# Turned x loaded for seven of eight tile pairs, and tile stores issued by ScalarE, in the front of a fused mixture kernel

## Chip, cores and metric

One Trainium2 chip, one core, one launch. The metric is the device time of the program in microseconds, as the median of several runs. Everything is float32 in memory. TensorE multiplies, VectorE (DVE), ScalarE (ACT) and GpSimd (POOL) do the rest; SyncE (SP) only issues transfers and waits.

## What is computed

```python
def reference(x, cond_128, ...):          # x: [32, 64, 1024], cond_128: [32, 128]
    x = x + L0_ffn(L0_cond(x, cond_128))
    x = x + L1_ffn(L1_cond(x, cond_128))
    return x

def L0_cond(x, emb):                      # mixes the 64 channels of a sample
    h = gelu(emb @ W0 + b0); h = gelu(h @ W1 + b1)
    att = softmax(h @ W2 + b2)            # [32, 8]
    agg_w = einsum('bk,koi->boi', att, weight); agg_b = att @ bias_k
    return einsum('boi,bih->boh', agg_w, x) + agg_b[:, :, None]

def L0_ffn(x):                            # 2048 rows of 1024, 8 experts, 2 of them per row
    topv, topi = top_k(x @ gate_w, 2); w = softmax(topv)
    return sum over the two experts e of w_e * (x @ expert_w[e])

def L1_cond(x, c):                        # grouped convolution, 9 taps, and c @ c_weight.T + bias
def L1_ffn(x):                            # x @ weight.T, and LoRA of 2 of 8 experts chosen by a gate
```

## The kernel before

The 2048 rows (32 samples of 64 channels) are 16 tiles of 128 rows, each with 1024 columns. The program has three parts: the **front** (0 to about 84 us of the profiled execution) mixes the channels, computes the gate, sorts every row into the lists of its two experts and stores the mixed rows in a scratch in DRAM (`c0_d`); the **expert slots** (92 to about 505 us) gather 128 rows of one expert at a time and multiply them with its weights, as three products of rounded parts (a low part of the rows with the high part of the weights, high with high, high with low; line 1498); the **second layer** takes the rest. The change touches the front and the first slot.

The front goes over pairs of tiles, `it` = 0 to 7; pair `it` has tiles `2*it` and `2*it + 1`. Nothing is scheduled by the compiler: each engine runs its own list of instructions in the order written, and they meet at semaphores.

- **x** comes twice. SyncE loads all 16 tiles as they are (`load_x`, line 453, 512 KB each, into `res`, read by the mixing). The gate needs x with columns on the partitions. For the pairs in `LOADED` (2 to 7) a copy turned on the host, `x_t`, is loaded (line 476, 1 MB a pair, into one of two buffers `xt_pair`, pair `it` in buffer `it % 2`). Pairs 0 and 1 are turned on chip: TensorE transposes a quarter of the pair into bank 4 (`turn_x`, line 1356), ScalarE copies it out (`take_turned`, line 755), and only then the next quarter may go in.
- **Prologue.** Three small matmuls with gelu and softmax make the attention (to line 931); TensorE spreads it over the partitions (line 1425), VectorE puts it in place (`att_own`, line 937), and 16 matmuls with `kern_sb` make the 32 mixing matrices in banks 0 to 3 (line 1442). VectorE (line 952) and ScalarE (lines 775, 778) copy them to `bd`, 4 copies each. Besides, lines 1428 to 1431 multiply the column sum of the gate, the context of the second layer and the bias. The column sum comes through `gsum`, the bias through a chain of four VectorE operations to `aggb` (line 948), which ScalarE needs for its first eviction of a mixed tile.
- **Gate.** `gate_products(it)` (line 1370) multiplies the turned pair with the gate's weights into bank 6; VectorE copies it (`take_rows`, line 961); `turn_gate` (line 1382) brings it back to rows, VectorE copies that (line 966), and `logits` (line 1401) mixes it.
- **Mixing.** `mix(it, j, h)` (line 1393) multiplies half `h` of tile `j` of the pair with its mixing matrix; ScalarE adds the bias while copying to `c0_sb[j]` (`take_c0`, line 764), and SyncE stores the tile (line 480).
- **Routing.** VectorE picks the two best logits (`route`), TensorE counts ranks (lines 1408, 1409), VectorE makes one-hot matrices (lines 990, 991), and `lists` (line 1417) adds up the row numbers of each expert's list.
- **Expert 0's weights** come beside this, one eighth in each pair (`load_raw0`, line 457), rounded by ScalarE (line 769), with the remainder taken by VectorE (`rest0`, line 1026).

TensorE's order in a pair is: the gate turn, mixing of tile 0 in two halves, logits, mixing of tile 1 in two halves, lists of the pair before, gate products of the pair after, ranks. In pair 0 the four quarters of pair 1's transposes stand between these.

SyncE's order sets when transfers start: all 16 tiles of x first, with two eighths of expert 0's weights between them; then, in each pair, the turned pair `it + 2` once the gate products of pair `it` have freed its buffer, the two stores once ScalarE has evicted, and an eighth of the weights.

Behind the last lists, GpSimd gathers the first 128 rows (`xg`, line 648), TensorE transposes them into banks 2 and 3 (line 1489), ScalarE rounds each half to `l_hi` (lines 797, 802), VectorE takes the remainder `l_lo` (lines 1086, 1091), and slot 0 begins.

## Time and profile before

| | us |
|---|---|
| median of the runs (807.08 to 810.27) | 807.54 |
| the profiled execution | 806.61 |
| its span in the profile | 804.9 |
| front, up to the first gather | 0 to 84.4 |
| first product of expert slot 0 | 92.0 |
| TensorE busy | 780.9 (97%) |
| VectorE busy | 393.6 (49%) |
| ScalarE busy | 206.3 (26%) |

The profile is one execution. Its page gives busy times of each engine and, in 40 slices, how busy they and the DMA engines were. The chain of waits goes back from the last instruction: at each step to what released it, or to the instruction before it on its engine. The timeline lists instructions in order of time, neighbours of one kind merged; in brackets stands how long the engine was idle before and what ended that. A matmul of float32 appears as two instructions. The granted clock is a separate column, in which 1.00 is full.

### The profile page before, as it was taken

The page shows a single profiled execution, that of the slowest core. Times are in us where ns is not written, and L with a number is a line of the kernel's source. Part 1 is how long each engine was busy: PE and PEld are TensorE (multiplying, and loading weights), DVE is VectorE, ACT ScalarE, POOL GpSimd, SP SyncE. Part 2 cuts the span into 40 slices and gives each one's busy share as a digit, 9 for nine tenths or more (in the row PEclk, how much of TensorE's full clock was granted, in tenths as well). Part 3 has the DMA queues.
Part 4 walks back from the last instruction along what each step waited for, and adds up shares of the span by engine and source line. Part 5 has one row for each costly group of instructions (what it writes and reads, how often), then busy time and mean ns, then how long its engine had stood idle before and what let it go on. Part 6 is the DMA issues. An engine that isn't in the chain of part 4 may idle for free.

```text
span 804.9 us, 13018 instructions
## 1 busy us (share of the span) xinstructions
PE 780.9 (97%) x4426; PEld 635.9 (79%) x4426; DVE 393.6 (49%) x920; ACT 206.3 (26%) x324; POOL 84.7 (11%) x127
## 2 busy tenths in 40 slices
PE   6999899899999999999999999999999999999997
PEld 4555587678787787877878888878988889889886
DVE  2688642330422413214133153475777667778883
ACT  3444152341523314224133251300000010001200
POOL 1000202001110110001011112211111111200000
PEclk9999999999999999999999999999999999999999
DMA  9997397376482765726455355774445654442066
GB/s 349 388 372 264 126 375 259 113 252 244 177 308 95 243 268 196 277 97 224 148 174 199 104 196 175 240 190 115 104 108 143 144 126 104 113 98 52 1 221 197
DMA packets 62880, 152.51 MB, mean 189 GB/s; under 512 B 7148, under 2 KB 24700, under 8 KB 61948
## 3 DMA queue, kind: packets, MB, share of 16 engines
q1 hardware_dynamic: 43152, 99.84, 38.0%
q0 software_dynamic: 9504, 34.48, 14.0%
q10 hardware_dynamic: 10188, 17.71, 5.9%
q8 instruction: 22, 0.36, 0.2%
q14 instruction: 14, 0.11, 0.1%
HBM read 99.04 MB, written 44.57 MB: 178 GB/s over the span
## 4 chain that ended last, share of the span: by engine, by line
PE 90%; DMA 5%; issue 2%; ACT 1%; DVE 1%; SPq 1%; POOLq 0%; POOL 0%; ACTq 0%; DVEq 0%
PE bank L1498 61%; PE bank L1586 6%; PE bank L1595 4%; PE bank L1393 3%; PE bank L1489 3%; PE bank L1541 3%; PE bank L1602 3%; DMA work<-c_scratch,idx 3%; PE bank L1370 1%; PE bank L1417 1%; PE bank L1552 1%; DMA work<-y_scratch,pos_c 1%; DMA x1p<-res 1%; PE bank L1356 1%; PE bank L1382 1%
## 5 line engine op out<-in xcount | busy, mean ns | idle before, releaser
L1498 PE MATMUL bank<-weights,l_hi 128*128 128x512 f32 x1536 | 473.5, 389 | 0.0
L1498 PEld LDWEIGHTS bank<-weights,l_hi 128*128 128x128 f32 x1536 | 288.4, 188 | 58.3
L1498 PE MATMUL bank<-weights,l_lo 128*128 128x512 f32 x768 | 304.7, 397 | 1.1 <-DVE l_lo L1086 1.1
L1498 PEld LDWEIGHTS bank<-weights,l_lo 128*128 128x128 f32 x768 | 144.2, 188 | 34.0 <-issue 6.2
L1086 DVE TENSOR_TENSOR l_lo<-bank,l_hi 128x512 fp32r<-128x512 f32 x32 | 22.2, 693 | 174.7 <-ACT l_hi L797 174.7
L1118 DVE TENSOR_TENSOR weights<-work,weights 128x1024 fp32r<-128x1024 f32 x48 | 55.9, 1221 | 33.9 <-ACT weights L809 33.9
L1586 PE MATMUL bank<-conv_sb,x1p 128*128 128x128 f32 x512 | 59.8, 275 | 2.7 <-DMA x1p<-res 1.6
L1586 PEld LDWEIGHTS bank<-conv_sb,x1p 128*128 128x128 f32 x512 | 58.7, 192 | 3.2 <-DMA x1p<-res 1.8
L1240 DVE TENSOR_TENSOR res<-bank,res 128x512 f32 (+1 forms) x30 | 31.9, 1064 | 54.8 <-PE bank L1498 43.8
L648 POOL DMA_INDIRECT work<-c_scratch,idx x32 | 33.4, 1045 | 227.1 <-PE bank L1489 138.8
L888 ACT ACTIVATE l_hi<-work 128x512 fp32r<-128x512 f32 x32 | 18.4, 623 | 135.4 <-PE bank L1498 129.2
L1091 DVE TENSOR_TENSOR l_lo<-bank,l_hi 128x512 fp32r<-128x512 f32 x32 | 22.1, 692 | 63.1 <-ACT l_hi L802 63.1
L809 ACT ACTIVATE weights<-work 128x1024 fp32r<-128x1024 f32 x48 | 47.2, 1046 | 18.7 <-issue 18.3
L797 ACT ACTIVATE l_hi<-bank 128x512 fp32r<-128x512 f32 x33 | 19.8, 599 | 98.0 <-PE bank L1498 88.5
L841 ACT ACTIVATE work<-bank 128x512 f32<-128x512 f32 x32 | 19.1, 596 | 87.4 <-PE bank L1498 69.0
L1595 PE MATMUL bank<-down_sb,work 128*128 128x160 f32 x256 | 37.4, 299 | 0.6 <-DVE hb L1206 0.6
L1192 DVE TENSOR_TENSOR work<-bank,ctxb 128x512 f32<-128x512 f32 x32 | 33.6, 1131 | 8.5 <-PE bank L1586 7.8
L1595 PEld LDWEIGHTS bank<-down_sb,work 128*128 128x128 f32 x256 | 36.2, 190 | 1.8 <-issue 0.8
L802 ACT ACTIVATE l_hi<-bank 128x512 fp32r<-128x512 f32 x33 | 19.7, 598 | 68.3 <-PE bank L1498 68.3
L1489 PEld LDWEIGHTS bank<-ca,work 128*128 128x128 f32 x264 | 30.8, 140 | 7.7 <-issue 2.2
L1489 PE MATMUL bank<-ca,work 128*128 128x128 f32 x264 | 34.4, 272 | 2.4 <-DMA work<-c_scratch,idx 2.4
L698 POOL DMA_INDIRECT work<-y_scratch,pos_c x32 | 32.8, 1026 | 26.2 <-POOL pos_c L693 9.7
(204 smaller groups left out, 603.6 us busy)
## 6 DMA issues: line engine op xcount, KB each, us to landing
work<-in_expert_w SPq DMA_DIRECT2D x52, 512.0 KB, 5.4
y_scratch<-work ACTq DMA_DIRECT2D x64, 256.0 KB, 3.4
x1p<-in_expert_w SPq DMA_DIRECT2D x20, 512.0 KB, 8.3
y_scratch<-ca SPq DMA_DIRECT2D x19, 512.0 KB, 10.1
res<-in_x SPq DMA_DIRECT2D x16, 512.0 KB, 11.2
c_scratch<-work SPq DMA_DIRECT2D x16, 512.0 KB, 5.0
res<-in_x_ph SPq DMA_DIRECT2D x14, 512.0 KB, 5.8
x1p<-res SPq DMA_DIRECT2D x112, 64.0 KB, 4.7
```

Of the source, the lines that this page charges most:

```text
L648: pool.indirect_dma_start(xg, None, c0_d, bass.IndirectOffsetOnAxis(ap=idx[:, 0:1], axis=0)).then_inc(s_xg, 16)
L698: pool.indirect_dma_start(yg[j][:, k, :], None, y_d, bass.IndirectOffsetOnAxis(ap=pos_c[j][:, k:k + 1], axis=0)).then_inc(s_yg[j][k], 16)
L809: act.activation(w_hi[1 - odd][:, at, :], raw[buffer(at)], ACT.Copy).then_inc(s_hi, 1)
L1118: dve.tensor_tensor(w_lo[1 - odd][:, at, :], raw[buffer(at)], w_hi[1 - odd][:, at, :].bitcast(F32), ALU.subtract).then_inc(s_lo, 1)
L1192: dve.tensor_tensor(out4[:, b], ps, add.unsqueeze(2).to_broadcast([P, CQ, HC, CP]), ALU.add).then_inc(s_c1, 1)
L1240: dve.tensor_tensor(to[:, w, :], bank[h][:, :].rearrange("p (w q) -> p w q", q=PH), rows[:, w, :], ALU.add).then_inc((s_me0, s_me1)[h], 1)
L1393: mm = pe.matmul(bank[2 * j + h][:, :], bd[:, t, :], x_sb[t][:, h * HALF:(h + 1) * HALF], start=True, stop=True)
L1489: mm = pe.transpose(bank[bk][:, k * P:(k + 1) * P], xg[:, at * P:(at + 1) * P], ident)
L1498: mm = pe.matmul(to[:, :], a[:, k, :], b[:, k, cols * HALF:(cols + 1) * HALF], start=(k == 0 and n == 0), stop=(k == HC - 1 and n == 2 and ...
L1541: mm = pe.matmul(bank[4][g * TAIL:(g + 1) * TAIL, 0:H // QUAD], tail_xt[:, TAILED.index(e), k, :], raw[buffer(k)][:, g * (H // QUAD):(g + ...
L1586: mm = pe.matmul(bank[to + b][:, at:at + P], x1p[j][:, b, u, m * P + k:(m + 1) * P + k], conv_sb[:, k, u, :], start=(k == 0), stop=(k == W ...
L1595: mm = pe.matmul(bank[2][:, 0:G1W], c1_of(t)[:, k, :], down_sb[:, k, :], start=(k == 0), stop=(k == HC - 1))
```

## The change

- `LOADED` gains pair 0, so `x_t` holds seven pairs. SyncE loads the constants and `kern_sb` first, then turned pair 0, then tiles 0 and 1 of x. Only pair 1 is still turned on chip.
- The turned pair 2 is requested between tiles 5 and 6 of x, where SyncE waits for the gate products of pair 0; the two eighths of expert 0's weights move from behind tiles 3 and 5 to behind tiles 7 and 9.
- The stores of mixed tiles leave SyncE's list. ScalarE issues each behind its eviction, after a wait for its own two writes.
- TensorE's prologue goes straight to the attention product, the kern products and the gate products of pair 0; the small matmuls come behind them, into bank 4, and the transposes of pair 1 wait until their results are read (`s_ctx0`). VectorE's and ScalarE's orders follow: the copies of `bd` first, then gate rows, `gsum`, `ctx0`, `aggb`.
- In every pair but the last, the first half of tile 0's mixing stands ahead of the gate turn, and in pair 0 the transposes of pair 1 move one place back. ScalarE evicts tile 0 of pair 0 before it takes any quarter.
- In slot 0 the first half adds up, for four blocks of 128 columns at a time, the products of the rounded rows with both parts of the weights, then those of the remainders.

```diff
-LOADED = [2, 3, 4, 5, 6, 7]
+LOADED = [0, 2, 3, 4, 5, 6, 7]
@@ SyncE
-            load_x(0)
+            def load_turned(it):
+                sp.dma_start(row(it % 2 * 2, 2), x_t[tile_rows(LOADED.index(it)), :]).then_inc(s_xtl[it % 2], 16)
+
             sp.dma_start(ca[:, mlp:CA_W], consts_a[:, mlp:CA_W]).then_inc(s_const, 16)
             sp.dma_start(kern_sb, kern.rearrange("p (o i) -> p o i", o=QUAD)).then_inc(s_kern, 16)
+            load_turned(0)
+            load_x(0)
             load_x(1)
...
             for t in range(2, NT):
                 load_x(t)
-                if t in (3, 5):
-                    load_raw0((t - 3) // 2)
+                if t == 5:
+
+                    sp.wait_ge(s_g, QUAD)
+                    load_turned(2)
+                if t in (7, 9):
+                    load_raw0((t - 7) // 2)
             for it in range(NT // 2):
-                if it + 2 in LOADED:
+                if it + 2 in LOADED and it > 0:
 
                     sp.wait_ge(s_g, (it + 1) * QUAD)
-                    n = LOADED.index(it + 2)
-                    sp.dma_start(row(it % 2 * 2, 2), x_t[tile_rows(n), :]).then_inc(s_xtl[it % 2], 16)
-                for j in range(2):
-
-                    sp.wait_ge(s_cev[j], 2 * (it + 1))
-                    sp.dma_start(c0_d[tile_rows(it * 2 + j), :], c0_sb[j]).then_inc(s_cst[j], 16)
+                    load_turned(it + 2)
@@ ScalarE
+                act.wait_ge(s_cev[j], 2 * (it + 1))
+                act.dma_start(c0_d[tile_rows(t), :], c0_sb[j]).then_inc(s_cst[j], 16)
...
-            for n in range(3):
-                take_turned(0, n)
-            act.wait_ge(s_pe0, 7)
-            for b in range(2):
-                act.activation(*block(QUAD - 2, b), ACT.Copy).then_inc(s_bda, 1)
-            take_turned(0, 3)
-            for b in range(2):
-                act.activation(*block(QUAD - 1, b), ACT.Copy).then_inc(s_bda, 1)
+            act.wait_ge(s_pe0, 5)
+            for g in range(QUAD // 2, QUAD):
+                for b in range(2):
+                    act.activation(*block(g, b), ACT.Copy).then_inc(s_bda, 1)
...
-                if not last:
-                    take_turned(it + 1, 0)
                 take_c0(it, 0)
                 if not last:
-                    for n in range(1, 4):
+                    for n in range(4):
                         take_turned(it + 1, n)
@@ TensorE, prologue
-            turn_x(0, 0)
-            turn_x(0, 1)
...
-            turn_x(0, 2)
-            turn_x(0, 3)
+            pe.wait_ge(s_const, 16)
             gate_products(0)
+            pe.wait_ge(s_gred, 1)
+            pe.matmul(bank[4][:, 0:E], ones, gl[:, :], start=True, stop=True)
+            pe.matmul(bank[4][0:B, CH:2 * CH], c("emb"), c("cw"), start=True, stop=True).then_inc(s_pe0, 1)
+            pe.wait_ge(s_attx, 1)
+            pe.matmul(bank[7][:, B * K8:2 * B * K8], c("ones", B), attx[:, :, :].rearrange("p n k -> p (n k)"),
+                      start=True, stop=True).then_inc(s_pe0, 1)
@@ TensorE, pairs
-                if not last:
-                    turn_x(it + 1, 0)
-                turn_gate(it)
+                if last:
+                    turn_gate(it)
                 mix(it, 0, 0)
                 if last:
                     logits(it)
+                else:
+                    turn_gate(it)
                 mix(it, 0, 1)
                 if not last:
-                    turn_x(it + 1, 1)
+                    turn_x(it + 1, 0)
                     logits(it)
                 mix(it, 1, 0)
                 if not last:
-                    turn_x(it + 1, 2)
+                    turn_x(it + 1, 1)
                 mix(it, 1, 1)
                 if not last:
+                    turn_x(it + 1, 2)
                     turn_x(it + 1, 3)
@@ TensorE, slot 0
+            def first_left_half():
+
+                for blocks, upper, lower in ((range(0, 4), s_ha, s_la), (range(4, HC), s_hb, s_lb)):
+                    pe.wait_ge(upper, 1)
+                    for k in blocks:
+                        for n, part in enumerate((w_hi[0], w_lo[0])):
+                            pe.matmul(bank[0][:, :], l_hi[:, k, :], part[:, k, 0:HALF], start=(k == 0 and n == 0), stop=False)
+                    pe.wait_ge(lower, 1)
+                    for k in blocks:
+                        mm = pe.matmul(bank[0][:, :], l_lo[:, k, :], w_hi[0][:, k, 0:HALF], start=False, stop=(k == HC - 1))
+                return mm
```

## Rows read from the trace of the kernel before

**Rows 1.** the page: engine totals, and GB/s of DMA in 40 slices

```profile
PE 780.9 (97%) x4426; PEld 635.9 (79%) x4426; DVE 393.6 (49%) x920; ACT 206.3 (26%) x324; POOL 84.7 (11%) x127
...
GB/s 349 388 372 264 126 375 259 113 252 244 177 308 95 243 268 196 277 97 224 148 174 199 104 196 175 240 190 115 104 108 143 144 126 104 113 98 52 1 221 197
```

**Rows 2.** chain of waits in order of time: start us, us, what

```profile
27.61 1.16 PE bank L1370 x16
...
35.10 1.10 PE bank L1370 x16
36.23 0.42 DVE ctxb L961
...
37.07 0.58 PE bank L1382 x4
...
42.52 1.10 PE bank L1370 x16
```

**Rows 3.** timeline, VectorE in the iteration of pair 2

```profile
42.04 1.23 DVE L1026 TENSOR_TENSOR weights<-x1p,weights 128x1024 fp32r<-128x1024 f32 x1
```

**Rows 4.** last loads of x: issue ns, first and last start; to landing

```profile
L454 SPq DMA_DIRECT2D res<-in_x x2: 1052/1058/1063, 12.7 to 13.7; - x2
...
DMA to landing us min/median/max: 15.8/15.9/16.0
```

**Rows 5.** the same for the x_t load of pair 3

```profile
L476 SPq DMA_DIRECT2D work<-in_x_t x1: 464/464/464, 29.0 to 29.0; - x1
...
DMA to landing us min/median/max: 8.1/8.1/8.1
```

**Rows 6.** stretches: busy by engine, clock, DMA share, GB/s

```profile
8.00:28.00 20.00, 17.66 (x110) 11.41 (x113) 6.15 (x27) 7.15 (x15) 0.00 (x0) 1.00 1.03 412
...
36.00:43.40 7.40, 6.96 (x48) 4.24 (x44) 6.47 (x32) 4.24 (x7) 0.00 (x0) 1.00 1.00 355
...
103.00:108.00 5.00, 5.00 (x24) 4.14 (x23) 1.97 (x3) 3.46 (x5) 0.00 (x0) 1.00 1.03 415
```

**Rows 7.** timeline, prologue: start us, us, engine, line, operation, idle before

```profile
7.69 0.21 DVE L931 COPY ctxb<-att 32x128 f32<-32x128 f32 x1
...
9.65 0.63 PE L1425 MATMUL bank<-ca,ctxb 32*128 32x32 f32 x2
...
10.21 0.60 PE L1428 MATMUL bank<-gl,ca 128*128 128x8 f32 x2
10.32 0.29 DVE L937 TENSOR_TENSOR ctxb<-bank,ca 128x128 f32<-128x128 f32 x1 [2.08 <-PE bank L1425]
...
11.63 0.59 PE L1442 MATMUL bank<-ctxb,work 32*128 32x128 f32 x3
...
17.55 1.90 PE L1370 MATMUL bank<-work,ca 128*8 128x256 f32 x16 [0.69 <-ACT work L755]
...
27.61 1.05 PE L1370 MATMUL bank<-work,ca 128*8 128x256 f32 x16 [0.78 <-ACT work L755]
```

**Rows 8.** ScalarE groups of the front: busy us, mean ns; idle before

```profile
L764 ACT ACTIVATE work<-bank,aggb 128x512 f32<-128x512 f32 x32 | 20.1, 685 | 29.0 <-PE bank L1393 21.3 <-DMA c_scratch<-work 7.6
...
L755 ACT ACTIVATE work<-bank 128x512 f32<-128x512 f32 x8 | 4.8, 594 | 11.3 <-PE bank L1356 11.3
```

**Rows 9.** small store issued by ScalarE: issue ns, start us; to landing

```profile
L780 ACTq DMA_DIRECT2D ctx_scratch<-ctx x1: 373/373/373, 16.9 to 16.9; - x1
...
DMA to landing us min/median/max: 5.1/5.1/5.1
```

**Rows 10.** timeline of SyncE: the stores of pair 1

```profile
35.17 1.48 SPq L480 DMA_DIRECT2D c_scratch<-work  x2
```

**Rows 11.** chain of waits ahead of expert slot 0

```profile
90.52 0.60 ACT l_hi L797
...
91.14 0.70 DVE l_lo L1086
...
91.98 0.47 PE bank L1498
```

More of the change, by code:

```diff
@@ L936, in _ @@
             dve.wait_ge(s_pe0, 4)
-            dve.tensor_tensor(att_own.rearrange("p (o n) -> p o n", o=QUAD), bank[6][:, 0:B].unsqueeze(1).to_broadcast([P, QUAD, B]),
+            dve.tensor_tensor(att_own.rearrange("p (o n) -> p o n", o=QUAD), bank[5][:, 0:B].unsqueeze(1).to_broadcast([P, QUAD, B]),
                               c("own").unsqueeze(2).to_broadcast([P, QUAD, B]), ALU.mult).then_inc(s_att, 1)
             dve.wait_ge(s_pe0, 5)
-            ch.add(dve.tensor_copy(gsum[:, :], bank[2][:, 0:E]))
-            dve.tensor_tensor(ctx0[:, :], bank[3][0:B, 0:CH], c("fside", B), ALU.add).then_inc(s_ctx0, 1)
+            for g in range(QUAD // 2):
+                for b in range(2):
+                    dve.tensor_copy(*block(g, b)).then_inc(s_bdv, 1)
+            dve.wait_ge(s_g, QUAD)
+            dve.tensor_copy(gt_sb[:, :], bank[6][:, 0:2 * P]).then_inc(s_gt, 1)
             dve.wait_ge(s_pe0, 6)
+            ch.add(dve.tensor_copy(gsum[:, :], bank[4][:, 0:E]))
+            dve.tensor_tensor(ctx0[:, :], bank[4][0:B, CH:2 * CH], c("fside", B), ALU.add).then_inc(s_ctx0, 1)
+            dve.wait_ge(s_pe0, 7)
             ch.wait()
@@ L948, in _ @@
             dve.tensor_reduce(aggb[:, :], aggb_q, AX.X, ALU.add).then_inc(s_aggb, 1)
-            dve.wait_ge(s_pe0, 7)
-            for g in range(QUAD // 2):
-                for b in range(2):
-                    dve.tensor_copy(*block(g, b)).then_inc(s_bdv, 1)
             dve.wait_ge(s_aggb, 1)
@@ L1019, in route @@
                 dve.wait_ge(s_m, it + 1)
-            take_rows(0)
             take_gate(0)
@@ L1350, in turn_x @@
                     pe.wait_ge(s_x[t], 16)
-                if it * 4 + n > 0:
+                if turned(it) * 4 + n > 0:
                     pe.wait_ge(s_xt, turned(it) * 4 + n)
+                else:
+                    pe.wait_ge(s_ctx0, 1)
                 for k in range(4):
@@ L1388, in mix @@
                 t = it * 2 + j
-                if h == 0 and it in LOADED:
+                if h == 0:
                     pe.wait_ge(s_x[t], 16)
@@ L1500, in product, with left_half @@
                 return mm
-            def slot(g, e, odd, first):
-                if first:
-                    pe.wait_ge(s_lo, (e + 1) * HC)
-                pe.wait_ge(s_e0, g + CREDIT)
+            def left_half(g, odd):
                 pe.wait_ge(s_la, g + 1)
@@ L1511, in slot @@
                     mm = product(k, bank[0], w_hi[odd], w_lo[odd], 0)
+                return mm
[8 more added lines that the diff above has]
+                        mm = pe.matmul(bank[0][:, :], l_lo[:, k, :], w_hi[0][:, k, 0:HALF], start=False, stop=(k == HC - 1))
+                return mm
+            def slot(g, e, odd, first):
+                if first:
+                    pe.wait_ge(s_lo, (e + 1) * HC)
+                pe.wait_ge(s_e0, g + CREDIT)
+                mm = first_left_half() if first and isinstance(e, int) and e == 0 else left_half(g, odd)
                 mm.then_inc(s_h0, 1)
```

11 lines of the change are left out of this document (2 added, 9 removed).

## Prediction, made before the changed kernel was run

> **What bounds the kernel now.** I read the page first: TensorE is busy 97% of the span, and DMA runs at 349 to 388 GB/s in the first three of 40 slices and mostly below 250 later [rows 1]. So only the front, the first 84 us, has a second limit beside TensorE. The chain of waits in order of time comes next. In the steady front, iterations repeat every 7.42 us (gate products of pair 2 at 35.10, of pair 3 at 42.52), and the chain changes engine at one place only: the gate products end at 36.20, VectorE copies them, and TensorE takes up pair 2 at 37.07 [rows 2]. Its own steps fill the rest. VectorE's timeline shows a second limit close behind: copy at 36.23, last operation of the iteration from 42.04 to 43.27, and nothing in between that waits for TensorE. That is 7.04 us of its own chain, with 0.38 us of wait before the next copy [rows 2, 3]. Last the transfers. The last load of x is issued at 13.74 and lands 16.0 us later, at 29.7; the turned pair 3, issued at 29.02, lands at 37.1 [rows 4, 5]. TensorE wants it at 42.52. So the loads have 5.4 us in hand, and the engines that carry them are full: their share is 1.03 from 8 to 28 us, at 412 GB/s, and 1.00 from 36 to 43.4 us [rows 6].
>
> **The change part by part.** Sums are made against the profiled execution, 806.61 us with a span of 804.9 us; the median of the runs is 807.54, so 0.9 us is added at the end.
>
> 1. Prologue. Before, the attention weights are ready at 7.90 (7.69 plus 0.21), but TensorE is at transposes and multiplies them at 9.65; VectorE spreads them at 10.32, and the kern products start at 11.63 behind four other matmuls [rows 7]. Afterwards nothing stands in front: product at 7.95, VectorE 0.67 later and 0.29 long, kern products at 9.05. They take 2.4 us (11.63 to about 14.0). Gate products of pair 0 follow with 1.9 us, as at 17.55, then the three small matmuls that took 10.21 to 11.63, 1.4 us: the first mixing matmul stands at 14.8 instead of 21.0. The bd copies of both other engines run beside the gate products.
>
> 2. Not all of these 6.2 us survives. The same gate products take 1.90 us at 17.55 and 1.05 us at 27.61 [rows 7], though the granted clock reads full in every stretch [rows 6]: TensorE starts at the lower of its two levels, 1.2 GHz, and is at 2.4 GHz later, by the spacing of its matmuls from about 21 us on. The mixing of pair 0 now falls into the slow part. From 14.8: two halves of mixing at 1.7 and 1.3 us, the small gate turn 0.8, ScalarE's eviction of tile 0 with its new wait and store issue 1.7 (two halves of 0.685, overlapped to 1.27, plus 0.1 plus the 0.35 to 0.37 that an issue takes on it [rows 8, 9]), and four evictions of 0.60 with three groups of transposes of 0.55 and the handovers between them, 4.8. That puts the gate products of pair 1 at 25.1 against 27.6: **2.5 us gained there**. With the fast clock from 17 us on it would be 3.3.
>
> 3. Steady order. With one mixing half (0.91 us) between the ranks and the gate turn, the wait for VectorE's copy is covered: 0.43 us. VectorE allows only 7.42 less 7.04, so an iteration takes 7.06 and **0.36 us is gained in each**, 0.4 at most. Below, if its copy of the gate result, which stands in that chain, has to wait for the later gate turn: nothing at all is gained.
>
> 4. Stores on ScalarE. Two issues and two short waits, 0.9 us an iteration, on an engine with 4.2 us of work in 7.4 [rows 6]: hidden. What is queued behind the issue is the take of the turned tile in pair 0's iteration (counted in 2) and the rounding of expert 0's weights, which VectorE reads an iteration later: hidden too. If the cover were gone, mixing of two pairs later would wait, 0.9 us at most. SyncE no longer stands behind evictions.
>
> 5. The transfers. One pair, 1 MB, is added. From 29.7 to 37.1 two pairs and two stores landed, 3 MB: 2.5 us for each MB [rows 4, 5]. The queue up to pair 3's turned tile therefore ends at 37.1 plus 2.5 for pair 0. But the stores of pair 1 used to be issued from 35.17 on [rows 10], behind it on SyncE's queue; now they go out at about 30.7 and 32.9 on ScalarE's own, and share the engines with loads that are still queued: 2.5 us more, 42.1. Those of pair 2, out at 37.7 and 39.9, may take up to 2.5 more, 44.6. How the engines divide between two queues the trace doesn't show for large transfers. A small store that ScalarE issued at 16.91 landed in 5.1 us [rows 9], where SyncE's load issued at 13.74 needed 16.0, so it isn't put behind the backlog. I take the middle, 43.35. TensorE would want pair 3 at 25.1 plus 2 times 7.06, 39.2. So it waits some 4 us, and this part is 0.9 us **later** than the 42.45 of before. Requesting pair 2 early, between tiles 5 and 6 of x, costs nothing: it lands at about 19, the backlog through x's sixth tile lasts until about 16 at 2.5 us for each MB, and SyncE waits for the gate products only until 13.4. It moves no byte out of the way of pair 3, since all of x stands ahead of that in both kernels.
>
>  The Trainium skill ("DMA: Bandwidth & Descriptors", Issuing engines are not separate DMA queues) says that transfers of all issuing engines run on the same 16 engines and interleave. By that rule the stores do take from the loads, 42.1 to 44.6 and not 39.6; the trace agrees as far as the small store's 5.1 us goes.
>
> 6. After pair 3 the debt is paid: pair 4's load, asked for at 33, lands at about 48, and is wanted at 50.4. Four iterations to pair 7 give back 4 times 0.36, 1.45 us.
>
> 7. Slot 0. ScalarE ends the first rounding at 91.12, VectorE the remainder at 91.84, the first product starts at 91.98 [rows 11]. Starting with products that need only the rounded half, 91.2: 0.75 us. The eight of them last 1.8 us, longer than VectorE's 0.70. Only the second gather isn't asked for earlier; if its rows come late, some of this is lost again: **0.75 us gained**, between 0.4 and 0.8.
>
> Sum: plus 0.9, minus 1.45, minus 0.75 is minus 1.3 us: 805.3 profiled, 806.2 as a median.
>
> **The rivals.**
>
> - *The transfers are not late.* Against it: item 5. For it: from 103 to 108 us three queues together reach 415 GB/s, while in 36 to 43.4 us one alone gives 355 at the same share [rows 6], so two queues may mix better, and the stores may get little of it. Then 2.5, six iterations of 0.36 and 0.75 count in full: 5.4 us, 802.1.
> - *The stores yield, but the load of pair 0 counts.* Pair 3 is there at 41 to 42, between the two: 804. It lies in the forecast's case.
> - *VectorE gives nothing back.* If the gate result reaches it late, the period stays 7.42 and 1.45 us is missing: 807.7.
> - *Slower: the wait cools TensorE.* Nowhere after the warm-up does the trace of before show it idle for over 1.6 us, and here it would stand still from 38 to 43 or 44. If it falls to 1.2 GHz, gate products cost 0.85 more, and each of four mixing halves as much again, some of it in VectorE's shadow: 2.5 us. With pair 3 at 44.6 that is 2.2 plus 2.5 minus 1.45 minus 0.75, 2.5 us slower: 810.0. If the mixed rate of 355 GB/s holds from 28 us on, pair 3 comes 1.6 us later still: 811.6. It decides from the point where the idle stretch is long enough for the clock to fall.
>
>  The Trainium skill ("TensorE: Matmul & The Clock Gate", What's actually happening) says that the slow clock is the resting state and that activity releases it. By that rule the stall of item 5 isn't paid once but twice, 810.0 and not 806.2; the trace shows the release between 17.55 and 27.61, and no stall long enough for the fall.
>
> **How the numbers follow.** Forecast 0.48, with its own range 804 to 808; transfers not late 0.27; VectorE gives nothing back 0.12; cooled 0.13. The likeliest gives 806.2. The range takes in the first rival with half a microsecond below it and the first form of the slower one: 801.5 to 810.0. About 0.5%, 4 us, is what a measurement of this kernel tells from no change. Faster than that is only the case in which the transfers are not late, nearly whole, 0.26. Slower is the second form of the last one, 0.06. The same: 0.68.
>
> **What would show it.** The kern products at about 9.1, and gate products of pair 0 at 11.4, show item 1; gate products of pair 1 at 25.1 item 2; a distance of 7.06 us between gate products from pair 4 on item 3. Item 5 shows as an idle stretch of TensorE ended by the load of a turned pair, at about 39 to 43; if there is none and pair 3's gate products start at 39, the first rival holds. The slow clock would show as gate products of 1.9 instead of 1.05 us behind that stretch. Slot 0's first product would stand one ScalarE rounding behind its transposes. The prediction is wrong as a whole if the transfers in flight at 30 to 42 us are fewer or quicker than the 2.5 us for each MB, or if stores wait on ScalarE's queue until the loads are through: then mixing of pair 3 would wait for evictions instead.

## The result, and the profile after

The changed kernel takes **813.12 us** (median of 8 runs, 810.78 to 816.41) against 809.64 us for the kernel before on the same chip (8 runs, 806.39 to 810.65). The ratio, taken over all runs, is 1.0054, with a 95% interval of 1.0033 to 1.0075; the medians alone stand 1.0043 apart. It is slower by half a per cent, where no change or a small gain was forecast. The profiled execution took 813.57 us with a span of 811.8 us.

The page of the changed kernel, engine totals, granted clock and GB/s in 40 slices of 20.3 us:

```profile
PE 784.3 (97%) x4410; PEld 636.0 (78%) x4410; DVE 392.6 (48%) x920; ACT 205.2 (25%) x320; POOL 84.2 (10%) x127
...
PEclk9989999999999999999999999999999999999999
...
GB/s 350 403 329 305 105 336 313 99 199 300 154 274 174 185 313 139 265 160 185 197 114 255 90 182 169 249 181 127 118 103 121 154 139 103 107 98 56 1 224 191
```

Against [rows 1] TensorE is busy 3.4 us longer with 16 matmuls fewer. So more than waiting was added: the same work ran slower somewhere. The third slice of the clock's row is the hint.

**The prologue does what was forecast.** Timeline of TensorE, changed kernel (start us, us, engine, line, operation; in brackets the idle time before):

```profile
8.02 0.63 PE L1426 MATMUL bank<-ca,ctxb 32*128 32x32 f32 x2 [1.06 <-DVE ctxb L930]
9.13 2.09 PE L1435 MATMUL bank<-ctxb,work 32*128 32x128 f32 x32 [0.47 <-DVE ctxb L936]
11.15 1.90 PE L1373 MATMUL bank<-work,ca 128*8 128x256 f32 x16
...
15.00 1.22 PE L1396 MATMUL bank<-res,bd 128*128 128x512 f32 x1
```

The kern products start at 9.13 and the first mixing at 15.0, where in the kernel before they stood at 11.63 and 21.0 [rows 7].

**Then the lead is lost at one place.** Chain of waits in order of time (start us, us, what):

```profile
26.26 1.17 PE bank L1373 x16
27.43 0.02 issue
27.45 17.05 DMA work<-in_x_t
44.50 0.14 issue
44.64 1.72 PE bank L1373 x16
...
47.33 1.89 PE bank L1396 x2
...
54.85 1.10 PE bank L1373 x16
```

Gate products of pair 1 start at 26.26, 1.35 us earlier than before [rows 2]; those of pair 3 at 44.64, 2.2 us later. Between stands the load of turned pair 3, requested at 27.45 and landed 17.05 us later; before it took 8.1 [rows 5]. Behind it, gate products take 1.72 instead of 1.10, and a mixing half (two matmul instructions) takes 1.89, where in pair 0's iteration of this kernel the slower of two at the full clock took 0.96. Gate products of pair 4 start 10.1 us after those of pair 3 (54.78 and 44.64), where the distance was 7.42.

Stretches of the changed kernel (window, its length, busy us of each engine, TensorE's granted clock, DMA share, GB/s):

```profile
0.00:44.50 44.50, 32.76 (x184) 19.61 (x184) 20.17 (x99) 17.33 (x31) 2.15 (x9) 1.00 0.96 381
...
39.90:44.60 4.70, 0.12 (x2) 0.00 (x0) 1.39 (x2) 2.21 (x4) 0.00 (x0) 1.00 1.02 425
...
44.90:51.70 6.80, 6.80 (x30) 3.65 (x22) 3.23 (x18) 1.06 (x1) 0.00 (x0) 0.50 0.91 371
...
51.70:54.80 3.10, 3.10 (x20) 2.02 (x20) 2.60 (x15) 2.07 (x4) 0.00 (x0) 1.00 0.35 139
...
54.80:61.60 6.80, 6.80 (x45) 4.14 (x44) 5.80 (x32) 3.54 (x6) 0.00 (x0) 1.00 0.87 316
```

TensorE stands still for 4.6 us while the DMA engines are full at 425 GB/s; then it works at half the clock, 1.2 GHz, for 6.8 us, and behind that the DMA engines are short of work (share 0.35 from 51.7 to 54.8). From pair 4 on an iteration takes 6.84 us with TensorE busy in all of it. For the kernel before the first stretch reads:

```profile
0.00:37.10 37.10, 28.73 (x177) 18.51 (x177) 14.67 (x71) 16.27 (x31) 2.15 (x9) 1.00 0.95 373
```

Until pair 3 has landed, 13.8 MB were moved before (373 GB/s times 37.1 us) and 17.0 MB after (381 times 44.5). The 3.1 MB more at 419 GB/s (the rate from 28 to 44.5 us) are 7.4 us, the whole delay from 37.1 to 44.5.

| start us, profiled execution | before | changed |
|---|---|---|
| gate products of pair 3 | 42.45 | 44.64 |
| of pair 4 | 49.9 | 54.8 |
| of pair 7 | 72.1 | 75.3 |
| first gather requested | 84.4 | 87.7 |
| transposes of slot 0 | 89.8 | 93.2 |
| transposes of the second 128 rows | 97.5 | 101.4 |
| transposes of the sixth | 158.7 | 165.4 |
| end of the span | 804.9 | 811.8 |

So 3.3 us come from the front, 0.5 from slot 0, and 2.9 us from a stretch around 137 us: the gather requested at 130.63 took 8.46 us, TensorE waited 2.2 us for it and then ran at the low clock from 140.4 to 143.9.

```profile
130.63 8.46 DMA work<-c_scratch,idx
139.13 1.09 PE bank L1489 x8
140.22 7.10 PE bank L1498 x24
```

This last part isn't in every profile, as the experiments show. The medians differ by 3.5 us and the ratio stands for 4.4 us, which is about the front's part and slot 0's, 3.8 us together. A low clock seems to be in every run of the changed kernel, though a mean doesn't say where: the mean granted clock of its eight runs lies between 0.988 and 0.994, that of the 28 runs of the kernel before that stand beside e5 to e8 between 0.992 and 1.000 with 0.9975 in the middle.

### The profile page after: what moved, and what is told of

The parts are those of the page before. It is cut to its first block, busy times and chain, and to the rows that moved or that the text cites. A ratio compares the mean times of both kernels' runs of the same rounds, so it can differ in the third digit from the quotient of the medians.

```text
span 811.8 us, 12983 instructions
## 1 busy us (share of the span) xinstructions
PE 784.3 (97%) x4410; PEld 636.0 (78%) x4410; DVE 392.6 (48%) x920; ACT 205.2 (25%) x320; POOL 84.2 (10%) x127
## 4 chain that ended last, share of the span: by engine, by line
PE 84%; DMA 9%; DVE 3%; issue 2%; ACT 1%; SPq 1%; POOLq 0%; POOL 0%; ACTq 0%; DVEq 0%
PE bank L1498 59%; PE bank L1603 6%; DMA work<-c_scratch,idx 5%; PE bank L1612 4%; PE bank L1489 3%; PE bank L1558 3%; PE bank L1619 3%; DMA work<-in_x_t 2%; PE bank L1396 2%; PE bank L1569 1%; DMA work<-y_scratch,pos_c 1%; PE bank L1373 1%; DMA x1p<-res 1%; SPq L591 1%; DVE weights L1026 0%
## 5 line engine op out<-in xcount | busy, mean ns | idle before, releaser
L796 ACT ACTIVATE l_hi<-bank 128x512 fp32r<-128x512 f32 x33 | 19.7, 597 | 104.2 <-PE bank L1498 92.2
L840 ACT ACTIVATE work<-bank 128x512 f32<-128x512 f32 x32 | 19.1, 596 | 85.6 <-PE bank L1498 72.1
L1489 PE MATMUL bank<-ca,work 128*128 128x128 f32 x264 | 34.5, 272 | 5.2 <-DMA work<-c_scratch,idx 5.2
L1396 PE MATMUL bank<-res,bd 128*128 128x512 f32 x64 | 37.1, 685 | 0.0
L801 ACT ACTIVATE l_hi<-bank 128x512 fp32r<-128x512 f32 x33 | 19.7, 597 | 67.9 <-PE bank L1498 67.9
## 6 DMA issues: line engine op xcount, KB each, us to landing
res<-in_x SPq DMA_DIRECT2D x16, 512.0 KB, 10.1
```

Of the source, the lines that this page charges most:

```text
L1396: mm = pe.matmul(bank[2 * j + h][:, :], bd[:, t, :], x_sb[t][:, h * HALF:(h + 1) * HALF], start=True, stop=True)
L1489: mm = pe.transpose(bank[bk][:, k * P:(k + 1) * P], xg[:, at * P:(at + 1) * P], ident)
```

## Experiments

Two theories carry the weight. **Bytes**: the DMA engines are full in the front, so whatever is moved ahead of a turned pair sets the earliest time of its gate products; the change adds bytes and also wants the pair earlier. **Cooling**: the wait this makes lowers TensorE's clock and costs a second time. The rivals: the stores' own queue is the cause; the new order of TensorE is; slot 0 is. All ratios are to the kernel before, run on the same chip. "Still" is the longest wait of TensorE between 25 and 80 us, "low clock" the stretches beginning before 100 us in which 0.5 was granted once it had been full; all times are of the profiled execution.

| kernel | ratio (95%) | pair 3 lands | its gate products | still | low clock | pair 7's gate products |
|---|---|---|---|---|---|---|
| before | 1 | 37.1 | 42.5 | 0.8 | none | 72.1 |
| changed | 1.0054 (1.0033 to 1.0075) | 44.5 | 44.6 | 4.6 | 44.9 to 51.7 | 75.3 |
| e1 stores back on SyncE | 1.0033 (1.0010 to 1.0056) | 40.6 | 47.5 | 7.1 | 33.0 to 46.6, 94.4 to 97.8 | 74.9 |
| e2 before, stores on ScalarE | 1.0042 (1.0018 to 1.0066) | 37.7 | 44.2 | 0.8 | none | 74.2 |
| e3 dummy matmuls in the wait | 1.0035 (1.0012 to 1.0057) | 44.7 | 44.8 | 3.7 | 43.2 to 56.8, 97.8 to 101.2 | 78.0 |
| e4 x behind the pairs | 0.9995 (0.997 to 1.002) | 34.5 | 39.9 | 1.8 | 51.6 to 58.5 | 74.9 |
| e5 before, order of pairs | 0.9963 (0.9941 to 0.9985) | 38.2 | 42.6 | 0.8 | none | 70.0 |
| e6 before, order of slot 0 | 0.9996 (0.9974 to 1.0017) | 37.6 | 40.9 | 0.8 | 90.5 to 93.9 | 70.6 |
| e7 half of late x left out | 0.9938 (0.9896 to 0.9981) | 34.4 | 39.9 | 0.8 | none | 67.7 |
| e8 before, both orders | 0.9972 (0.9939 to 1.0004) | 38.1 | 42.7 | 0.8 | none | 70.1 |
| e9 before, order and stores | 0.9994 (0.9971 to 1.0018) | 37.2 | 41.9 | 1.3 | 92.6 to 96.0 | 72.4 |
| e10 e1 and e4 together | 0.9968 (0.9942 to 0.9993) | 34.3 | 36.9 | 2.2 | 57.1 to 60.5 | 70.7 |
| e11 order, and 3 MB more | 1.0059 (1.0039 to 1.0079) | 46.2 | 46.3 | 2.7 | 46.6 to 53.5 | 77.1 |

### e1: the changed kernel with its stores back on SyncE

```diff
@@ SyncE, in each pair behind load_turned
+                for j in range(2):
+                    sp.wait_ge(s_cev[j], 2 * (it + 1))
+                    sp.dma_start(c0_d[tile_rows(it * 2 + j), :], c0_sb[j]).then_inc(s_cst[j], 16)
@@ ScalarE, take_c0
-                act.wait_ge(s_cev[j], 2 * (it + 1))
-                act.dma_start(c0_d[tile_rows(t), :], c0_sb[j]).then_inc(s_cst[j], 16)
```

> The changed kernel with one part undone: SyncE issues the stores of mixed tiles again, behind the turned load of the same pair, as before the change; all else as changed. Theory S (stores on ScalarE's own queue take the DMA engines from the loads that SyncE still has queued): the load of turned pair 3 lands at about 39.6 us (37.1 of before plus 2.5 for pair 0) instead of 44.5, gate products of pair 3 start at 40 instead of 44.6, TensorE never stands still for over 2 us in the front and its clock stays full; pair 3 to pair 4 takes about 6.9 us instead of 10.1, and the whole is 6 to 8 us faster than the changed kernel, ratio to before 0.993 to 0.997. Rival B (the added 1 MB and the order of the loads alone make pair 3 late): it still lands after 42.5, the stall and the slow clock stay, ratio 1.000 to 1.005.

Pair 3 lands at 40.6, so taking the stores off the second queue brought it forward by 3.9 us (pair 4's load, too, is requested only at 40.4 here and at 34.9 in the changed kernel). That the wait would go was expected too, but it moves forward instead. Waits between 20 and 50 us (who waited for what: us, times, longest):

```profile
ACT work L771 <- DMA c_scratch<-work: 12.6, 1, 12.6
...
PE bank L1398 <- ACT work L771: 7.1, 1, 7.1
```

The stores of pair 0 were issued at 20.3 and 23.4, behind all of x and turned pair 2, and landed at 36.9 and 38.2. ScalarE can't evict the next tile into the same `c0_sb` until then, and the mixing waits for ScalarE. The queue of the stores isn't the cause by itself; it chooses who waits for the full engines. The low clock came here too, at 33.0, inside the wait. The ratio, 1.0033, can't be told from the changed kernel's; the intervals overlap.

### e2: the kernel before with only its stores moved to ScalarE

```diff
@@ SyncE
-                for j in range(2):
-                    sp.wait_ge(s_cev[j], 2 * (it + 1))
-                    sp.dma_start(c0_d[tile_rows(it * 2 + j), :], c0_sb[j]).then_inc(s_cst[j], 16)
@@ ScalarE, take_c0
+                act.wait_ge(s_cev[j], 2 * (it + 1))
+                act.dma_start(c0_d[tile_rows(t), :], c0_sb[j]).then_inc(s_cst[j], 16)
```

> The kernel before with one part of the change alone: ScalarE issues the stores of mixed tiles. Theory S: turned pair 3 lands at 39.6 to 42 us instead of 37.1, since the stores of pair 1 go ahead of it, which is still inside the 42.5 us at which it is wanted; no stall or one under 1 us, ratio to before 0.999 to 1.003. Rival B: landing stays at 37.1 us, ratio 1.000. If the stores gain anything by themselves, ratio below 0.998.

Slower by 0.4%, above what was expected, and no wait for a transfer explains it: pair 3 is in time. Its profile is only 1.9 us longer than the one before: 1.7 us appear in the iteration of pair 0, where the clock rose at 23.2 instead of 20.9, and 0.4 us between pairs 6 and 7. Some 0.5 of the 1.7 us belong to the stores: in e9, where they are on ScalarE too and the clock rose at 20.9, pair 0's gate products and pair 1's are 10.55 us apart, against 10.06 before. In the front, ScalarE waits longer for stores:

```profile
ACT work L760 <- DMA c_scratch<-work: 17.8, 7, 5.5
```

It was 7.6 us in all before [rows 8]. But between 22 and 84 us only 0.3 us of TensorE's waits are for those evictions, so **where most of the 0.4% lies stays open**.

### e3: dummy matmuls in the wait

```diff
+                if it == 3:
+                    keep_warm(5, ones, ca[:, 0:HALF])
                 if it in LOADED:
```

> The changed kernel with five extra matmuls of 128x512 whose results nobody reads, put ahead of the gate products of pair 3, where TensorE stands still for 4.6 us. Theory C (the stall costs twice, since TensorE falls to the lower clock behind it): gate products of pair 3 still start at 44.6 us, but pair 3 to pair 4 takes 6.9 us instead of 10.1, so the whole is 3.3 us faster than the changed kernel, ratio to before 1.000 to 1.002. Rival: the 10.1 us come from late transfers or from VectorE; then they stay and the ratio stays at 1.004 or 1.005.

This doesn't decide on cooling: the matmuls ended at 41.0, TensorE was idle for another 3.7 us, and the clock fell all the same, at 43.2, inside that wait. The ratio, 1.0035, is above the 1.000 to 1.002 of theory C, and its interval overlaps the changed kernel's. Two stretches of this kernel:

```profile
41.00:44.70 3.70, 0.03 (x1) 0.00 (x0) 0.00 (x0) 0.00 (x0) 0.00 (x0) 0.79 1.03 428
44.70:57.50 12.80, 12.73 (x48) 7.09 (x52) 6.55 (x32) 3.44 (x5) 0.00 (x0) 0.53 0.67 264
```

It shows something else. Here the clock rose at 12.4 and pair 1's gate products stood at 23.0, 3.3 us earlier than in the changed kernel; pair 3's came at 44.8, as there. **TensorE's lead is worth nothing** ahead of a landing that the bytes fix.

### e4: x tiles 10 to 15 requested behind the turned pairs

```diff
-            for t in range(2, NT):
+            for t in range(2, 10):
                 load_x(t)
...
                     load_turned(it + 2)
+                    for t in range(8 + 2 * it, min(10 + 2 * it, NT)):
+                        load_x(t)
```

> The changed kernel with another order of the loads: tiles 10 to 15 of x are requested behind turned pairs 3, 4 and 5, two tiles each, instead of all ahead of pair 3; the bytes are the same and the stores stay on ScalarE. Theory Q (pair 3 is late because 3 MB that are wanted 10 us and more later stand ahead of it in the queue): it lands at 37 us, gate products of pair 3 start at about 40, no stall, clock full, 7 to 8 us faster than the changed kernel, ratio to before 0.992 to 0.996. Rival: the engines are short of bandwidth over the whole front, so the stall only moves to pair 5 or 6, and the ratio stays above 1.000.

Pair 3 lands at 34.5, earlier than expected, its gate products stand at 39.9 as expected, and the half per cent is gone; the gain of 0.992 to 0.996 that was expected didn't come. Pair 7 is hardly earlier than in the changed kernel (74.9 and 75.3), for the same bytes are now missed by the stores. So in the profiles most of the 3.4 us between the two spans isn't in the front: 0.5 us are there at the first gather (87.18 and 87.71), and 2.3 us come from the gather requested at about 130 us, for which TensorE waits only 1.5 us here, with no low clock behind it. Waits between 22 and 84 us, then those of TensorE between 40 and 80 us:

```profile
ACT work L769 <- DMA c_scratch<-work: 24.0, 9, 4.0
```

```profile
PE bank L1398 <- ACT work L769: 3.9, 3, 1.8
```

A store takes 7.4 to 8.2 us to land between 40 and 60 us, longer than the iteration of 6.84, and each `c0_sb[j]` has one store per iteration.

### e5: the kernel before with only the order of pairs 1 to 6

```diff
-                turn_gate(it)
+                if it == 0 or last:
+                    turn_gate(it)
                 mix(it, 0, 0)
                 if last:
                     logits(it)
+                elif it > 0:
+                    turn_gate(it)
                 mix(it, 0, 1)
```

> The kernel before with one part of the change alone: from pair 1 to pair 6 the first half of tile 0's mixing stands ahead of the gate turn. No byte is added and SyncE keeps the stores. Theory D (in the front the DMA engines are the second bound: turned pairs have 5 us in hand in the kernel before, and each gain of TensorE's is free until these are used up): the distance between gate products falls from 7.42 to 6.84 us, as in the changed kernel where nothing waits, pair 7's gate products start at 68.6 to 69.5 us instead of 72.1, ratio to before 0.995 to 0.998. Rival E (the buffers of the mixed tiles bind already: a store lands 6 us after its issue, and with the eviction that is a cycle of 7.4 us): the distance stays above 7.2 us, and the ratio is 0.999 to 1.001.

Faster than the kernel before, 0.9963, with an interval clear of 1. The stretch from pair 1's gate products to pair 7's in this kernel, and in the kernel before:

```profile
28.90:70.00 41.10, 41.07 (x267) 25.02 (x269) 36.37 (x190) 20.64 (x31) 0.00 (x0) 1.00 0.96 362
```

```profile
27.60:72.10 44.50, 41.87 (x264) 25.45 (x264) 37.89 (x192) 21.27 (x32) 0.00 (x0) 1.00 0.94 355
```

TensorE has no idle time left in six iterations, and they are 3.4 us shorter (pair 7's gate products stand at 70.0, half a microsecond behind the expected range). Pair 3 lands at 38.2 for 42.6: there were 5.4 us in hand, and this order takes 0.9 us of it.

### e6: the kernel before with only the order of slot 0

```diff
+            def first_left_half():
...
+                mm = first_left_half() if first and isinstance(e, int) and e == 0 else left_half(g, odd)
```

> The kernel before with one part of the change alone: the order of the products in the first half of slot 0. If the first product may start when the rounded half is there, it stands 0.35 to 0.75 us earlier and the ratio is 0.999 to 1.000; if the second gather takes that back, 1.000. It would be above 1.001 only if the other order of the products itself cost something.

Nothing to be measured, 0.9996. In its profile the slot begins at the low clock (the same eight matmuls took 2.06 us in the changed kernel):

```profile
89.96 3.31 PE L1517 MATMUL bank<-weights,l_hi 128*128 128x512 f32 x8 [0.72 <-ACT l_hi L797]
```

### e7: the changed kernel with fewer bytes

Tiles 6 to 15 of x get only their first 512 columns; the other half is zeros, so 2.6 MB aren't moved. TensorE, VectorE and ScalarE run the same instructions, but for one wait of TensorE for the zeros.

```diff
             def load_x(t):
-                sp.dma_start(x_sb[t], x[tile_rows(t), :]).then_inc(s_x[t], 16)
+                w = HALF if t >= 6 else H
+                sp.dma_start(x_sb[t][:, 0:w], x[tile_rows(t), 0:w]).then_inc(s_x[t], 16)
```

> The changed kernel with part of the computation left out: of tiles 6 to 15 of x only the first 512 columns are loaded, and the mixing reads zeros in the other half; the gate, and with it the lists of rows, are as before. That takes 2.6 MB out of SyncE's queue and nothing else. Theory D: turned pair 3 lands at about 38.5 us (44.5 less 2.5 us for each MB) and no wait for it is left, all distances between gate products are 6.84 us, the clock stays full, pair 7's gate products start at 67.3 us, and the kernel is 7 to 8 us faster than the changed one: ratio to before 0.993 to 0.997. Rival F (the time is lost to the ScalarE queue, the evictions or VectorE): gate products of pair 3 stay near 44 us and the ratio stays above 1.002.

0.9938, with pair 3 landed at 34.4, 4 us earlier than expected. Two stretches, which cover the time of the changed kernel's wait:

```profile
28.00:36.00 8.00, 8.00 (x51) 4.88 (x50) 7.20 (x40) 4.30 (x6) 0.00 (x0) 1.00 0.92 334
36.00:43.40 7.40, 7.40 (x46) 4.46 (x46) 6.81 (x36) 3.59 (x5) 0.00 (x0) 1.00 0.96 380
```

TensorE is never idle in them and the clock stays full; pair 7's gate products stand at 67.7 instead of 75.3, though pair 1's stand where they did, at 26.24. The bytes alone decide between 1.0054 and 0.9938, of which the front has 7.6 us: theory Bytes. The stores are on ScalarE here and the order is the new one, so neither is the cause by itself.

### e8: the kernel before with both orders

> The kernel before with two parts of the change together, the steady order of pairs 1 to 6 and the order of the products in slot 0: those that neither add nor move a transfer. Theory D: 2.5 to 4 us faster than before, ratio 0.995 to 0.997. Rival E: ratio 0.999 to 1.001.

Its edit is that of e5 and e6 together. 0.9972 beside e5's 0.9963: slot 0's order adds nothing that can be measured.

### e9: the kernel before with the order of pairs and the stores on ScalarE

Its edit is that of e5 and e2 together.

> The kernel before with the order of pairs 1 to 6 (half of tile 0's mixing ahead of the gate turn) and the stores on ScalarE; pair 0 isn't loaded turned, prologue and slot 0 as before. Theory D (bytes ahead of a turned pair set a floor): pair 3 lands at 38 as in the kernel with the order alone (38.2) and is wanted at 28.9 + 2 x 6.84 = 42.6, so no stall and no fall of the clock at pair 3. The order gives 0.4%, the stores take 0.4%: ratio 0.998 to 1.003. Rival (the stores on ScalarE make the stall, whatever is loaded): pair 3 lands after 43 and TensorE stands still over 1.5 us there, ratio over 1.004.

0.9994, and pair 3 lands at 37.2: no wait for it, and no low clock among the pairs. So the order and the stores don't make the changed kernel's wait without the bytes of pair 0 and the earlier prologue, and the stores on ScalarE cost about the order's gain. The 0.3% between e5 and e9 is at the edge of what the intervals tell apart, but e10 against e4 (0.9968 and 0.9995) points the same way. Part of that cost shows in this profile, in TensorE's waits between 42 and 82 us (e5 has no such line):

```profile
PE bank L1391 <- ACT work L760: 2.6, 4, 1.3
```

### e10: the changed kernel with both repairs, e1 and e4

> The changed kernel with both repairs: x tiles 10 to 15 requested behind the turned pairs 3, 4 and 5, and the stores back on SyncE. If each debt has its own queue: pair 3 lands by 34.5, TensorE's distance stays 6.84, gate products of pair 7 at about 67.4 and ratio 0.994 to 0.997. Theory D: the bytes of the front (one MB more than before) need their time whatever the order, a stall of 1 us or more shows at stores or at x tiles between 45 and 70 us, gate products of pair 7 at 71 to 75, ratio 0.997 to 1.002.

0.9968: better than the kernel before, level with e5, and at the border between the two expected ranges; pair 7's gate products, at 70.7, are outside both. The clock rose at 12.7 here, which put pair 1's at 22.6. The debt is still there, as waits of 2.2 and 1.7 us for stores at 46 and 55 us, and gate products of pair 7 at 70.7, 3 us later than where the bytes are missing (e7):

```profile
PE bank L1400 <- ACT work L773: 3.8, 2, 2.2
```

### e11: e5 with 3 MB more ahead of pair 3

Of the change, this has the order of pairs only; it loads six tiles of x a second time.

```diff
+                    if it == 1:
+                        for t in range(10, NT):
+                            sp.wait_ge(s_x[t], 16)
+                            load_x(t)
                     sp.dma_start(row(it % 2 * 2, 2), x_t[tile_rows(n), :]).then_inc(s_xtl[it % 2], 16)
```

> The kernel before with the order of pairs 1 to 6, and six tiles of x (3 MB) loaded a second time ahead of turned pair 3; nothing else of the change. It compares with the order alone (0.9963, pair 3 landing at 38.2, wanted at 42.6). Theory D at 2.5 us for each MB: pair 3 lands at 38.2 + 7.5 = 45.7, TensorE stands still for 3 to 4 us before it. If a wait of that length lowers the granted clock (theory C), 0.5 shows for 5 to 14 us behind it, 3 us more are lost, gate products of pair 4 come 10 us after those of pair 3, and the ratio is 1.001 to 1.006. If lateness is all, 0.999 to 1.001 at most. If bytes are not what sets the landing, pair 3 lands before 42 and the ratio stays 0.996.

Bytes alone rebuild the changed kernel's loss: 1.0059, from e5's 0.9963. Pair 3 lands 8.0 us later than in e5, 2.7 us for each MB. (Its request is 4.3 us later too, since SyncE waits for each of the six tiles before it loads it again; but the DMA engines don't stand idle, with a share of 0.96 or more from 28 us on.) Chain of waits, then two stretches:

```profile
34.65 11.54 DMA work<-in_x_t
46.20 0.14 issue
46.33 1.66 PE bank L1374 x16
...
48.96 2.02 PE bank L1397 x2
...
56.61 1.10 PE bank L1374 x16
```

```profile
43.60:46.30 2.70, 0.00 (x0) 0.00 (x1) 1.28 (x2) 0.00 (x0) 0.00 (x0) 1.00 0.94 378
46.60:53.40 6.80, 6.80 (x29) 3.61 (x22) 3.17 (x18) 3.37 (x5) 0.00 (x0) 0.50 1.04 405
```

A wait of 2.7 us, and 0.5 granted for 6.8 us behind it; pair 4 comes 10.2 us after pair 3, nearly the changed kernel's 10.1. A late pair 3 costs its lateness, 3.7 us against e5, and another 3.4 us (10.2 less 6.84) for the clock. That is theory Cooling, with nothing else of the change but the order in the kernel.

## Why the prediction was wrong

It forecast 806.2 us with 801.5 to 810.0; the chance of slower by over 0.5% was put at 0.06. The change is 0.54% slower. (The kernel before ran at 809.64 beside it, not at 807.54; scaled to 807.54 the change would be at 811.0 by the medians and at 811.9 by the ratio, outside the range as well.) The step that failed is 6, the debt "paid" after pair 3 with the clock left at full; 5 and 7 were mis-sized. In the terms of its sum, for the profiled execution:

| term | forecast | measured |
|---|---|---|
| 5. gate products of pair 3 | +0.9 | +2.2 |
| 6. from there to pair 7 | -1.45 | +1.0 |
| 7. slot 0 | -0.75 | +0.5 |

1. **Prologue: right.** Kern products at 9.13 (said 9.05), gate products of pair 0 at 11.15 (11.4), first mixing at 15.0 (14.8).

2. **Gate products of pair 1: right in kind, too large.** They start at 26.26, a gain of 1.35 us and not 2.5, with the clock rising at 21.0 as assumed (by the spacing of the matmuls; the column of the granted clock reads 1.00 before that, too). The mis-sized term is the first: both mixing halves and the gate turn, 3.8 us by the forecast, took 4.7 (15.0 to 19.7), each half about 2.1. What follows was right: 1.7 us to the first quarter's copy at 21.42, 4.8 from there. The moment of the rise isn't a property of the kernel, though: with the same prologue the clock rose at 12.4 to 12.7 in the profiles of e1, e3 and e10, which had pair 1 at 22.3 to 23.0; with the old prologue it rose between 15.4 and 26.1.

3. **Steady order: right, but the gain was put too small.** 6.84 us from pair 4 on, not 7.06, and e5 gives the gain by itself. The wrong term is VectorE's chain of 7.04 us, taken as a bound. It was read from a copy that had waited for TensorE to the end of the last operation. Where the copy needn't wait, it starts 0.09 us before the operation ahead of it ends, and the next one follows it by 0.33 us and not 0.44. Timeline of VectorE in e5:

```profile
49.62 1.23 DVE L1026 TENSOR_TENSOR weights<-work,weights 128x1024 fp32r<-128x1024 f32 x1
50.76 0.42 DVE L961 COPY ctxb<-bank 128x256 f32<-128x256 f32 x1
51.09 0.25 DVE L973 TENSOR_TENSOR rk<-oh,bank 128x16 f32<-128x16 f32 x2
```

 So the chain takes 0.2 us less when it runs without a wait: e5's copies start at 43.92, 50.76 and 57.61, 6.84 us apart (7.02 once), and VectorE keeps up with TensorE.

4. **Stores on ScalarE, "hidden": wrong.** e2 costs 0.42% and e9 against e5 about 0.3%. The cover named was ScalarE's idle time; what was missing is that ScalarE waits for its own stores, and that mixing waits for ScalarE. In e9 this accounts for most of it: 2.6 us of TensorE's waits, and some 0.5 us in pair 0's iteration. In e2, where TensorE's waits for ScalarE from 42 to 82 us are only 0.3 us, most of it isn't located.

5. **Transfers: the mechanism right, the size too small.** It added pair 0 and the stores of pair 1, 42.1, let the stores of pair 2 take up to 2.5 us more, 44.6, and then took the middle of 42.1 and 44.6 for no reason from a row. Pair 3 landed at 44.5, after 3.1 MB more. DMA queues of the changed kernel up to 44.5 us (packets, MB, share), then of the kernel before up to 37.1; q1 is SyncE's, q10 ScalarE's:

```profile
q1 hardware_dynamic: 3702, 14.76, 84.4%
q10 hardware_dynamic: 637, 2.16, 11.9%
```

```profile
q1 hardware_dynamic: 3704, 13.82, 94.7%
```

 The 2.16 MB are the four stores of pairs 0 and 1 (2.10 MB) and hardly any of pair 2's, which went out at 40.9 and 44.3, later than assumed. The third megabyte is on SyncE's own queue: it had given up two stores and taken on pair 0, which are alike, and yet moved 0.94 MB more. By the size of the packets in the trace some 0.75 MB of that are of pair 4's load, requested at 34.9 behind pair 3 (37.2 before), and moved in part ahead of it. So the upper bound came true partly by luck, with other bytes than those listed. The Trainium skill ("DMA: Bandwidth & Descriptors", Issuing engines are not separate DMA queues) says that transfers of all issuing engines interleave; the trace agrees, with 2.16 MB of stores moved beside the loads. The conclusion, a wait of 4 us (measured 4.6), was right; that pair 3 would come only 0.9 us later wasn't, 2.2 were measured.

6. **The debt "is paid" after pair 3: wrong.** Pair 4 comes 10.1 us after pair 3. The rival "the wait cools TensorE", given 0.13, is what happened, priced at 2.5 us where 3.3 was measured (10.1 less 6.84), the more since mixing and lists were hit as well as gate products. With both lateness and cooling it said 810.0, the range's upper end; from its own start of 806.61 plus 2.19 of lateness, 2.72 more up to pair 4 and 1.74 back from three shorter iterations, the front gives 809.8 for the profiled execution, and the 0.75 us of slot 0 don't come off it; with slot 0 and the gather at 130 us it was 813.57. The rival's 1.6 us for a mixed rate of 355 GB/s don't follow from its rows either: what 412 GB/s move from 28 to 44.6 us would take 2.7 us more at 355. e11 confirms the mechanism. In the profile before, no wait was longer than 1.6 us, and one of 4 us was itself forecast: a fall of the clock deserved more than 0.13. The Trainium skill ("TensorE: Matmul & The Clock Gate", What's actually happening) says that the slow clock is the resting state; 0.5 granted from 44.9 to 51.7, right behind the wait, agrees.

7. **Slot 0: 0.75 us promised, none measured** (e6, e8). From the transposes to the first product 1.76 us pass where it was 2.13, a gain of 0.37. The timeline of the changed kernel shows how even that goes:

```profile
94.98 2.06 PE L1517 MATMUL bank<-weights,l_hi 128*128 128x512 f32 x8 [0.70 <-ACT l_hi L796]
...
101.38 1.10 PE L1489 MATMUL bank<-ca,work 128*128 128x128 f32 x8 [0.71 <-DMA work<-c_scratch,idx]
```

 The second gather is requested by GpSimd 2.8 us after the first has landed, whatever TensorE does, and here took 5.4 us (4.3 before). The prediction named this risk and kept the gain.

**What stays open.** For the gather requested at 124 to 131 us TensorE waits over 2 us in five profiles (changed 2.2, e1 3.4, e6 2.6, e8 2.6, e10 2.4), and the low clock follows in three of them (changed, e6, e8), not in e1 and e10. From the second gather's transposes to the sixth's that costs 2.5 to 3.2 us against the kernel before in changed, e1, e6 and e8, and 1.4 in e10. All five have slot 0's new order, but three others with it (e3, e4, e7) don't show the wait, nor do the five without it; no run tells chance from cause. And 0.4% for the stores on ScalarE alone (e2) is measured but mostly not located. What decides whether the clock falls behind a wait is open as well (below).

## What to carry to other kernels

Where the DMA engines are full, ask of each load how many bytes are moved before it lands, over all queues and with the stores, and set the landing against the moment it is wanted; moving a request to another queue or place first of all chooses who waits: e1 and e4 leave pair 7's gate products at 74.9 us (75.3 in the changed kernel), and only both together bring them to 70.7, in a profile with an early rise of the clock. An edit that makes the consumer earlier and one that adds bytes eat the same reserve from both sides, so they must be judged together: here the new order alone is worth 0.4% (e5), and the earlier prologue bought with 1 MB more, with the stores on ScalarE, turns that into a loss. A wait of some microseconds on TensorE must be priced with the clock that it can lose behind it: 3.3 and 3.4 us more behind 4.6 and 2.7 us here. And a chain read off an engine that waits in each iteration is longer than the same chain run without the wait, by 0.2 of 7.04 us here.

## What the runs showed of the hardware

- 0.5 was granted behind waits of 2.2 us (at 137 us of the changed kernel, for 3.4 us), 2.7 us (e11, 6.8 us) and 4.6 us (changed, 6.8 us), and from inside waits of 3.7 us (e3, 13.7 us) and 7.1 us (e1, 13.7 us). In the kernel before, whose longest wait is 1.6 us, it stayed at 1.00 up to 802.6 us. It isn't a matter of length alone. There was none behind a wait of 3.4 us at 137.3 in e1, nor behind 2.2 us at 46.0 and 2.4 us at 131.1 in e10. But e4 shows 6.8 us of it behind a wait of 1.6 us at 49.0, and e1, e3, e6 and e9 show 3.4 us of it behind waits of 1.3 to 1.6 us for slot 0's gather, where the kernel before waits 1.4 us and stays at full.
- When the clock first rises varies between profiles of kernels with the same prologue, 15.4 to 26.1 us and 12.4 to 21.4 us, and moves pair 1's gate products by up to 4 us.
- A second queue hardly adds to the rate: 425 GB/s with the stores on a second queue (39.9 to 44.6), 428 in e3, against 412 from one queue at 8 to 28 us of the kernel before [rows 6] and 423 at 28 to 34, all on SyncE's queue. (The 415 of [rows 6] come from three queues.) The 355 GB/s of mixed transfers in [rows 6] was not a limit of mixing.
- A store of 512 KB took between 2.6 and 8.0 us to land when ScalarE issued it (changed kernel) and between 2.6 and 9.5 when SyncE did (before): the long ones are those among queued loads, on either queue.
